# Loading each 1 MB adjacency block of a two-layer graph kernel as two 512 KB transfers

## The reference

```
x = layernorm(x + adj @ (x * (u >= 0.1) / 0.9))
s = adj @ expmap(x)                 # expmap: tanh(|x|) * x / |x|, row by row
x = layernorm(x + logmap(s) @ kernel + bias)   # logmap: arctanh(min(|s|, 0.999)) * s / |s|
```

## Time and profile before

| | |
|---|---|
| time, median of 3 runs | 946.2 us (946.13 to 947.37) |
| time of the profiled execution | 946.4 us |
| its span in the profile | 944.2 us |
| granted TensorE clock, mean | 0.994 of full speed |
| PE busy | 898.7 us, 95% of the span |
| read from HBM, written | 355.57 MB, 2.10 MB |

### The profile page before, as it was taken

The page is one execution under the profiler, slowest core; times in us unless marked ns, Lnnn a source line. Parts: engine busy times, 40 slices in busy tenths (PEclk is TensorE's granted clock), DMA queues, the critical chain, the costliest instruction groups (busy, mean ns, idle before and its releaser), DMA issues.

```text
span 944.2 us, 10549 instructions
## 1 busy us (share of the span) xinstructions
PE 898.7 (95%) x4224; PEld 322.4 (34%) x4224; DVE 283.0 (30%) x1046; ACT 53.2 (6%) x138; POOL 56.9 (6%) x49
## 2 busy tenths in 40 slices
PE   5669999999999999999999999999999999999993
PEld 1113333333333333333333444444444444443331
DVE  1134574322314130304040221203121030336644
ACT  0000110000000000000000000000000000013322
POOL 0000000000000000000000000000000000003322
PEclk9999999999999999999999999999999999999997
DMA  9999999999999999997979998997989979899992
GB/s 369 414 421 420 421 421 420 421 422 421 421 421 421 421 417 422 380 423 258 424 237 413 390 363 320 341 423 283 407 290 370 422 269 362 336 423 421 421 422 108
DMA packets 53328, 358.35 MB, mean 380 GB/s; under 512 B 6305, under 2 KB 8353, under 8 KB 10401
## 3 DMA queue, kind: packets, MB, share of 16 engines
q1 hardware_dynamic: 50544, 355.49, 93.4%
q10 hardware_dynamic: 2736, 2.20, 0.7%
HBM read 355.57 MB, written 2.10 MB: 379 GB/s over the span
## 4 chain that ended last, share of the span: by engine, by line
PE 83%; DMA 7%; DVE 3%; SPq 2%; ACT 2%; POOL 1%; issue 1%; ACTq 0%; POOLq 0%; DVEq 0%
PE sums_both L629 38%; PE sums_first L583 20%; PE sums_part L592 16%; DMA ring<-adj_dram 7%; PE sums_part L583 4%; PE sums_both L611 3%; PE sums_part L611 3%; SPq L313 1%; ACT xres L363 1%; POOL rooted L330 1%; DVE stats L425 1%; SPq L309 1%; DVE y L541 1%; SPq L308 0%; DVE mv L428 0%
## 5 line engine op out<-in xcount | busy, mean ns | idle before, releaser
L629 PE MATMUL sums_both<-ring,feats 128*64 128x512 f32 x1696 | 370.3, 592 | 0.5 <-DMA ring<-adj_dram 0.5
L583 PE MATMUL sums_first<-ring,feats 128*64 128x512 f32 x1088 | 246.6, 599 | 28.4 <-DMA ring<-adj_dram 28.4
L629 PEld LDWEIGHTS sums_both<-ring,feats 128*64 128x64 f32 x1696 | 136.7, 137 | 228.0 <-issue 226.0
L592 PE MATMUL sums_part<-ring,feats 128*64 128x512 f32 x880 | 193.3, 593 | 0.0
L583 PEld LDWEIGHTS sums_first<-ring,feats 128*64 128x64 f32 x1088 | 78.8, 138 | 189.3 <-issue 140.1
L435 DVE TENSOR_TENSOR row_saved<-sums_both,row_saved 64x512 f32<-64x512 f32 x15 | 10.2, 683 | 349.3 <-ACT row_saved L383 349.2
L592 PEld LDWEIGHTS sums_part<-ring,feats 128*64 128x64 f32 x880 | 66.9, 137 | 119.0 <-issue 118.2
L340 POOL TENSOR_TENSOR rooted<-base,power 128x8 f32<-128x8 f32 x16 | 27.8, 1735 | 795.7 <-DVE base L462 795.7
L492 DVE TENSOR_TENSOR support<-sums_part,support 128x512 f32<-128x512 f32 x36 | 24.9, 692 | 139.2 <-PE sums_part L592 139.1
L583 PE MATMUL sums_part<-ring,feats 128*64 128x512 f32 x208 | 48.5, 595 | 2.8 <-DMA ring<-adj_dram 2.8
L383 ACT COPY row_saved<-sums_first 64x512 f32<-64x512 f32 x16 | 9.3, 580 | 600.4 <-PE sums_first L583 600.4
(11 more groups left out here) (64 smaller groups left out, 236.1 us busy)
## 6 DMA issues: line engine op xcount, KB each, us to landing
ring<-adj_dram SPq DMA_DIRECT2D x335, 1024.0 KB, 12.9
xres<-x_dram SPq DMA_DIRECT2D x8, 256.0 KB, 17.0
support<-u_dram SPq DMA_DIRECT2D x8, 256.0 KB, 16.8
out_dram<-xres ACTq DMA_DIRECT2D x16, 128.0 KB, 7.5
selw<-selector_dram ACTq DMA_DIRECT2D x1, 32.0 KB, 3.4
selw<-weight_dram ACTq DMA_DIRECT2D x1, 32.0 KB, 3.7
bias_sb<-bias_dram ACTq DMA_DIRECT2D x1, 32.0 KB, 6.1
```

The source lines that it names most:

```text
L583: last = nc.tensor.matmul(bank[at:at + F], feats[:, c * TB + t, which, :], ring[:, slot, t, :], start=start and t < 2, stop=stop and t >= ...
L592: last = nc.tensor.matmul(bank[F * g:F * g + F], feats[:, c * TB + t, 1, :], ring[:, slot, t, :], start=start and t == 0, stop=stop and t ...
L629: last = nc.tensor.matmul(sums_both[r % 2][layer * F:layer * F + F], feats[:, c * TB + t, layer, :], ring[:, slot, t, :], start=begin and ...
```

## The change

Each block is loaded as two transfers of 512 KB: the first brings tiles 0 and 1 of every partition and counts on `block_loaded`, the second brings tiles 2 and 3 and counts on a new semaphore `rest_loaded` of the same slot. A transfer still has 128 runs, now of 4 KB each, 8 KB apart in DRAM and in the ring. SP waits for the release once, before the first of the two. PE starts a step when the first halves of its blocks are there, and waits for the second halves in front of its third tile (t = 2), in all four places where blocks are multiplied. The release of a block, the order of the steps and the transfers of `x` and `u` are unchanged.

```diff
@@ -258,6 +258,7 @@
         early_banks = [sums_both[0], sums_part[PARTS - 1]]
 
         block_loaded = [sem(f"block_loaded{i}") for i in range(SLOTS)]
+        rest_loaded = [sem(f"rest_loaded{i}") for i in range(SLOTS)]
         chunk_loaded = [sem(f"chunk_loaded{i}") for i in range(NT // CHUNK)]
         params_loaded = sem("params_loaded")
         dropped = sem("dropped")
@@ -310,7 +311,9 @@
                 if released:
 
                     sp.wait_ge(block_released, released)
-                sp.dma_start(ring[:, slot], adj[r, c]).then_inc(block_loaded[slot], 16)
+                for part, loaded in enumerate((block_loaded, rest_loaded)):
+                    t = slice(part * TB // 2, (part + 1) * TB // 2)
+                    sp.dma_start(ring[:, slot, t, :], adj[r, c, :, t, :]).then_inc(loaded[slot], 16)
 
         @block.gpsimd
         def _(pool):
@@ -576,9 +579,16 @@
         def _(pe):
             finished = 0
 
+            def rest_of(i):
+
+                for slot, nth in uses[i][0]:
+                    pe.wait_ge(rest_loaded[slot], 16 * nth)
+
             def two_halves(bank, which, slot, start, stop):
 
                 for t in range(TB):
+                    if t == TB // 2:
+                        rest_of(i)
                     at = F * (t % 2)
                     last = nc.tensor.matmul(bank[at:at + F], feats[:, c * TB + t, which, :],
                                             ring[:, slot, t, :],
```

## The result

| | before | after |
|---|---|---|
| median | 947.37 us (5 runs, 946.13 to 948.3) | 957.37 us (5 runs, 956.87 to 959.18) |
| ratio | | 1.011, 95% interval 1.0096 to 1.0123 |
| span of the profiled execution | 944.2 us | 955.0 us |

Forecast were 952.2 us, 5.8 over the profiled 946.4, so the direction was right and the loss, 10.0 us between the medians, was about 1.7 times the forecast one.

What follows compares the result with a forecast made beforehand. Loads were taken to bound the beginning and end, PE the middle. Added time of +4.2 us at the beginning and +1.7 at the end, on the profiled 946.4 us, gave 952.2 us, range 946 to 959.

Steps and rivals of the forecast that it cites:

- What bounds the kernel: Whole kernel: late loads set the time at the beginning and the end, PE alone sets the pace in between.
- So the 92nd decides: Beginning: of the loads PE waits for, the 92nd sets PE's delay, +4.2 us; the 107th would ask only +3.1.
- The price of the runs, p: Every block load: 4 KB runs in place of 8 KB add 0.055 to 0.068 us, taken as 0.065.
- The gain of the halves: Where loads bound: starting on the first half ends a step of 8 matmuls 1.28 us earlier, of 4, 0.86.
- PE's waits, taken as nothing: Each PE step: one or two more waits in its middle, hidden in PE's queue, cost zero.
- The beginning, +4.2 us: Up to the 92nd load: 6.0 us later, less 1.28 for the first half and 0.54 of cushion.
- the 92nd load lands 92 x 0.065 = 6.0 us later: Beginning: each of the first 92 loads adds 0.065 us, delaying the 92nd by 6.0 us.
- the costs taken as nothing, point 2: SP's queue: 335 more issues at 0.50 us each cost zero, as 13 halves in flight still hold 16 us of DMA time.
- at 421 GB/s without a dip: First 16 slices, up to some 378 us: the DMA was read as running steadily at 421 GB/s.
- The end, +1.7 us: From 827 us on: 39 blocks take 2.5 us longer, and the last step gives back 0.86.
- 39 x 0.065: End: the 39 blocks left in the saturated stretch each take 0.065 us more, 2.5 us together.
- The sum: Whole kernel: beginning and end together +5.8 to 5.9 us on the profiled 946.4, giving 952.2 us.

Runs made afterwards that it cites:

- experiment 8: Changed kernel with only the 23rd, 76th, 77th, 81st, 92nd and last three loads halved, all others whole: 945.78 us, ratio 0.9985 to the kernel before.
- Experiment 2: Kernel before with each block's halves apart in DRAM: still one transfer per block, but of 256 runs of 4 KB; ratio 1.0093, 8.8 us over the kernel before.
- experiment 4: Changed kernel, but transfers cut into even and odd partitions, 64 runs of 8 KB each, both awaited at step start: ratio 1.0014 to the kernel before.
- experiment 1: Changed kernel with PE waiting for both halves at the start of each step, not in mid-step: 959.85 us, ratio 1.0136 to the kernel before.

## Why the prediction was right in direction and short in size

1. **What bounds the kernel.** Right in the main. Loads set the time at the beginning and again at the end, PE in between: the delay stays at 6.5 us from 291 to 846 us, and experiment 8 gains just by halving loads at these places. "So the 92nd decides" was not right: in the profile of the kernel after 6.0 of the 6.45 us are there from the second half of the 81st load on.
2. **The price of the runs, p = 0.055 to 0.068, taken 0.065.** Right: 2.557 - 2.488 = 0.069 us. Experiment 2 shows that it is the runs, experiment 4 that it isn't the transfers. Fitted from the 256 KB transfers of x and u, whose runs are 2 KB, it held for 4 KB. Of the two figures of the Trainium skill, page "DMA: Bandwidth & Descriptors", the stream of 4 KiB rows at 408.7 GB/s (section "SWDGE vs HWDGE vs iDMA") agrees with the 409 measured here. The 3 cycles per packet (section "Why small descriptors are slow") would give, as an estimate, 0.03 us, under half of the 0.069 measured.
3. **The gain of the halves, 1.28 + 0.86 us.** Right within the noise: experiment 1 loses some 2.5 to 4.0 us without it, where 2.1 were forecast.
4. **PE's waits, taken as nothing.** Right: x64 in 13.73 us.
5. **The beginning, +4.2 us.** Short by 2.2. The term that failed is the first product, "the 92nd load lands 92 x 0.065 = 6.0 us later": it took the added time as p per load from the first load on. The 23rd load was already 3.7 us later in place of 1.6, and from there to the 77th the loads kept to 2.556 us. What was left out is in the costs taken as nothing, point 2: the reasoning on SP's queue asked only whether enough bytes are in flight. There were enough, and yet the engines moved 241 GB/s from 4 to 6 us and 375 from 6 to 8. The start of the DMA was not looked at: "at 421 GB/s without a dip" passes over the 369 of the first slice of the earlier trace rows, which is now 340. Over the kernels that begin with halves (76.66, 75.67, 76.12 and 76.37 us for the 23rd load) and those that begin with 23 whole blocks (72.97, 73.70, 72.81, 72.78 and 73.27) the difference is 3.1 us, so the start's own loss is 1.5 us beyond the 1.6 of the runs. Another 0.3 is 92 x 0.003, by which p was taken too low, and the last 0.4, which in this profile come at the 92nd and the 107th load, are within what two executions of the kernel before differ by here (839.85 and 841.17 us for the first small product).
6. **The end, +1.7 us.** Short by 2.6. Some 1.2 of it, about half, is the good profile of before: its last load took 88.3 us, where the same kernel took 90.5 in another execution and experiment 8's, whole from the 93rd to the 332nd load, 89.7. Against the mean of these three, 89.5, the four kernels with halves throughout or from the fifth load (93.5, 93.6, 93.0, 93.4) need 3.9 us more, 1.2 over the price of the runs. The price itself, "39 x 0.065", is borne out by the pace of 409 GB/s and not by this stretch alone: experiment 2, which pays it, needs 2.8 us more than the first profile of before and 1.6 more than the mean, and the three of that mean lie 2.2 us apart. So whether the 1.2 are a loss of the halves or the spread of single executions is open.
7. **The sum again.** With p = 0.068 it is 6.2 us; with 1.5 for the start and 1.2 for the end 8.9. Measured were 10.4 and 8.9, with intervals of about 1.3 us each way; as the two terms were read from the same profiles, that fit is no test of them. The failure is in size: a loss of some 1.5 us by the 23rd load that the forecast put at nothing, one of 1.2 at the end whose cause and place are not settled, and the sum's footing on one profiled execution that was a short one.

What stays open is why halves lose time at the start, and where exactly at the end. The start's dip needs both small runs and many transfers (each alone gives 348 and 331 GB/s from 4 to 6 us, near the 342 of the kernel before in its second execution; both together give 241), it isn't ACT's parameter traffic, and it isn't a lack of issued bytes: at 3.56 us SP had issued 2.6 MB, and up to 6 us some 1.1 MB were moved. Which part of the DMA's path is late then, these runs don't show.

## What to carry to other kernels

Before a transfer is cut, look in the trace for two transfers with runs of different lengths: two durations give the price of a run, and the count of loads in the saturated stretches (here 92 and 39 of 335) tells what of it reaches the end. In this kernel cutting paid only for loads for which the consumer really stood waiting; 8 of 335 loads gave 1.4 us, and all 335 lost 9 to 10. And where two profiles are compared at single places, take a second profile of the same kernel first: at the end of this one two executions of the same program differed by 2.2 us.

## What the runs showed of the hardware that was not expected

Two transfers that fill 64 neighbouring partitions each, 8 KB a partition, ran at 229 GB/s with a DMA share of 1.02; the even and the odd partitions, 64 as well, ran at 421.

The granted clock of PE fell in two stretches of the kernel after, 32 to 40 and 60 to 74 us, in which PE waited for loads. Windows of the kernel after:

```profile
32.00:40.00 8.00, 5.76 (x18) 1.40 (x16) 1.95 (x4) 0.00 (x0) 0.00 (x0) 0.79 1.03 405
60.00:62.00 2.00, 0.70 (x2) 0.20 (x4) 1.92 (x7) 0.00 (x0) 0.00 (x0) 0.87 1.04 418
62.00:64.00 2.00, 2.00 (x8) 0.56 (x6) 1.83 (x12) 0.00 (x0) 0.00 (x0) 0.50 1.02 406
64.00:74.00 10.00, 8.90 (x34) 1.78 (x32) 2.56 (x10) 0.21 (x1) 1.68 (x1) 0.95 1.03 410
```

In the profile of before the clock is 1.00 throughout these stretches, with PE idle for 0.55 us before a step of 1.9; after, it works 1.08 us and idles 0.2. Between 62 and 64 us the mean is 0.50, which is 1.2 GHz in place of 2.4. PE had idled for 1.7 us before 61.30 us, and its next 20 matmul instructions took 6.21 us in one piece; as loads were the bound there, this cost nothing that the next steps show: from 67.71 us on they start 1.28 us apart again. The short pieces are not shown to be the cause. In the kernel with halves only from the 24th load on, which works in steps of 1.9 us there, the granted clock was 0.66 from 20 to 24 us, after PE had idled for 2.32 us; and in the second execution of the kernel after it was 1.00 from 60 to 64 us.
